# Fetched expert rows turned by column-quarter DMAs and a VectorE transposition, with two smaller edits on TensorE's transposes

## The reference

```python
probs = jax.nn.softmax(x @ router_w, axis=-1)            # 8 experts
gates, idx = jax.lax.top_k(probs, 2)
gates = gates / jnp.sum(gates, axis=-1, keepdims=True)
...
g = jax.nn.silu(x @ w_gate[e]); u = x @ w_up[e]           # for each expert e, 768 x 768
expert_out = (g * u) @ w_down[e]
routed = sum over the two experts of gate * expert_out
shared = jax.nn.silu(x @ ws_gate) * (x @ ws_up) @ ws_down
return alpha * shared + (1.0 - alpha) * routed
```

## Time and profile before

| what | value |
|---|---|
| median of three runs | 1616.88 us |
| time of the profiled execution | 1615.58 us |
| its span | 1613.9 us |
| TensorE busy | 1534.7 us (95%) |
| VectorE busy | 813.6 us (50%) |
| ScalarE busy | 347.2 us (22%) |
| GpSimd busy | 254.3 us (16%) |
| mean granted clock of TensorE | 0.992 of full speed |
| mask blocks | about 477 us to 503 us |
| expert tiles | about 1018 us to 1598 us |

### The profile page before, as it was taken

The page is one execution under the profiler, slowest core; times in us unless marked ns, Lnnn a source line. Parts: engine busy times, 40 slices in busy tenths (PEclk is TensorE's granted clock), DMA queues, the critical chain, the costliest instruction groups (busy, mean ns, idle before and its releaser), DMA issues.

```text
span 1613.9 us, 21893 instructions
## 1 busy us (share of the span) xinstructions
PE 1534.7 (95%) x8432; PEld 1019.5 (63%) x8433; DVE 813.6 (50%) x1534; ACT 347.2 (22%) x525; POOL 254.3 (16%) x236
## 2 busy tenths in 40 slices
PE   5999999999999899999989999899999999999996
PEld 3566676558889899999886555444444444444442
DVE  8655558997677899976897243111111111111111
ACT  3321121112231346550481210110000000001000
POOL 1187820000000000000000047011111111111111
PEclk9999999999999999999999999999999999999998
DMA  9900010000023426213202337924628211613450
GB/s 256 361 2 2 2 62 1 1 1 2 1 60 98 129 76 200 50 25 85 56 23 61 145 88 155 320 92 164 225 79 297 92 49 54 214 40 117 150 204 21
DMA packets 85338, 163.80 MB, mean 101 GB/s; under 512 B 18874, under 2 KB 48816, under 8 KB 85001
## 3 DMA queue, kind: packets, MB, share of 16 engines
q1 hardware_dynamic: 66903, 119.07, 22.9%
q0 software_dynamic: 12096, 23.27, 6.4%
q10 hardware_dynamic: 6258, 20.40, 4.5%
HBM read 127.75 MB, written 37.56 MB: 102 GB/s over the span
## 4 chain that ended last, share of the span: by engine, by line
PE 68%; DVE 11%; POOL 7%; issue 5%; DMA 5%; DVEq 1%; SPq 1%; ACT 1%; POOLq 0%
PE bank L817 30%; PE bank L1641 7%; POOL slot_table L1339 7%; PE bank L1679 6%; PE bank L1600 4%; PE bank L1543 4%; PE bank L727 2%; DVE arena L2412 2%; PE bank L1481 2%; PE bank L737 2%; DVE arena L2381 2%; PE bank L755 2%; PE bank L1727 1%; DMA arena<-in_L_ffn_w_down_dram 1%; DVE arena L2357 1%
## 5 line engine op out<-in xcount | busy, mean ns | idle before, releaser
L817 PE MATMUL bank<-arena 128*64 128x384 f32 x3312 | 539.7, 487 | 3.4 <-DMA arena<-in_L_ffn_w_down_dram 2.8
L817 PEld LDWEIGHTS bank<-arena 128*64 128x64 f32 x3312 | 236.7, 137 | 294.7 <-issue 290.2
L1179 DVE SCALAR_TENSOR_TENSOR arena<-bank,arena 64x384 f32<-64x384 f32 x88 | 50.3, 610 | 356.5 <-DMA arena<-out_dram,arena 216.8
L1679 PE MATMUL bank<-arena 125*125 125x198 f32 (+1 forms) x1200 | 189.2, 318 | 10.6 <-DVE arena L2381 10.5
L1679 PEld LDWEIGHTS bank<-arena 125*125 125x125 f32 x1200 | 182.9, 193 | 14.9 <-DVE arena L2381 14.7
L1641 PE MATMUL bank<-arena 128*125 128x192 f32 x960 | 163.4, 328 | 0.5 <-DVE arena L2334 0.5
L1641 PEld LDWEIGHTS bank<-arena 128*125 128x125 f32 x960 | 157.5, 189 | 0.8 <-DVE arena L2334 0.8
L2221 DVE TENSOR_TENSOR arena<-arena,bank 125x417 f32 x186 | 109.6, 589 | 43.4 <-PE bank L1481 36.2
L1339 POOL DMA_INDIRECT slot_table<-arena x80 | 111.9, 1399 | 93.2 <-issue 93.2
L1543 PE MATMUL bank<-arena 128*125 128x396 f32 x240 | 96.2, 496 | 0.0
L900 ACT ACTIVATE arena<-bank 128x384 f32<-128x384 f32 x46 | 22.6, 492 | 337.0 <-PE bank L817 337.0
(11 more groups left out here) (307 smaller groups left out, 1556.4 us busy)
## 6 DMA issues: line engine op xcount, KB each, us to landing
arena<-in_L_ffn_w_gate_dram SPq DMA_DIRECT2D x9, 2304.0 KB, 8.9
arena<-in_L_ffn_w_up_dram SPq DMA_DIRECT2D x9, 2304.0 KB, 10.8
arena<-in_L_ffn_w_down_dram SPq DMA_DIRECT2D x9, 2304.0 KB, 8.9
arena<-score_rows ACTq DMA_DIRECT2D x18, 585.9 KB
expert_in<-arena SPq DMA_DIRECT2D x23, 384.0 KB, 10.3
arena<-expert_in ACTq DMA_DIRECT2D x23, 384.0 KB, 3.3
arena<-in_L_mix_w_qkv_dram SPq DMA_DIRECT2D x2, 2304.0 KB, 17.7
xn_columns<-arena SPq DMA_DIRECT2D x1, 3750.0 KB, 15.7
```

The costliest lines, as they stand in the source:

```text
L817: ins = tp.matmul(ps[bank][HP * h:HP * h + HP, 0:384], frm[:, b, k, HP * h:HP * h + HP], ew[h][i][:, k, n * 384:(n + 1) * 384], start=(k = ...
L1679: ins = tp.matmul(ps[bank][0:T, c * width:(c + 1) * width], ptile[0:T, j % NPT, dt * T:(dt + 1) * T], values(n - first, st), start=(st == ...
```

## The change

1. **Rows of the experts.** For tiles 1 to 22 the rows are no longer transposed by TensorE. `load_x` issues four DMAs instead of one. DMA number c brings column quarter c (192 columns) of all 128 rows to the 32 partitions 32c to 32c+31; row 32i+r goes to partition 32c+r, place i. One VectorE instruction (`turn_x`) then transposes all 32x32 blocks and writes `xgT` whole. What lands on partition p are then the six features 6p to 6p+5, so the gate and up matrices are laid out in the same way (`"(p k) n -> p k n"`: six consecutive rows of a matrix on a partition, 18 KB in one piece). Down keeps its layout. Tile 0 is still transposed by TensorE, with every sixth column as a piece, and its load is cut in four DMAs by rows. ScalarE's copies of the transposes go.
2. **Transposes of h.** TensorE does those of i=0 inside the second half of the up product (before k=3), and those of i=1 inside the down product (before k=1).
3. **Mask blocks.** ScalarE writes the counts in bf16; TensorE multiplies 125x128 pieces of them with a bf16 identity instead of transposing f32. The three last rows of each result hold other counts and aren't read. VectorE makes the bf16 identity once (one 128x128 copy).

Some semaphores are joined; this moves nothing.

```diff
@@ ffn_sync: the experts' matrices
+        ROWS_OF = ("(p k) n -> p k n", "(p k) n -> p k n", "(k p) n -> p k n")
...
-                sp.dma_start(ew[b][i], w[(NE - 1) * b].rearrange("(k p) n -> p k n", p=P)).then_inc(s_ew[i], 16)
+                sp.dma_start(ew[b][i], w[(NE - 1) * b].rearrange(ROWS_OF[i], p=P)).then_inc(s_ew[i], 16)
...
-                                 w[bass.ds(e, 1)].rearrange("e (k p) n -> p (e k) n", p=P)).then_inc(s_ew[i], 16)
+                                 w[bass.ds(e, 1)].rearrange(("e (p k) n -> p (e k) n", "e (p k) n -> p (e k) n",
+                                                             "e (k p) n -> p (e k) n")[i], p=P)).then_inc(s_ew[i], 16)
@@ ffn_pe: tile
-                pe.wait_ge(s_xTs, 2 * j + 2)
+                if isinstance(j, int) and j == 0:
+                    pe.wait_ge(s_xTs, 2)
+                else:
+                    pe.wait_ge(s_xTd, j)
                 for m in range(2):
                     pe.wait_ge(s_ew[m], loads)
                     for i in range(2):
                         for k in range(KD):
+                            if (m, i, k) == (1, 1, 3):
+                                h_transposes(j, b, 0)
                             ins = product(2 * m + i, xgT, b, k, m, i)
                         ins.then_inc((s_g, s_up)[m], 1)
-                h_transposes(j, b, 0)
-                if not (isinstance(j, int) and j == NTM - 1):
-                    x_transposes(j + 1, 1 - b)
-                else:
+                if isinstance(j, int) and j == NTM - 1:
...
-                h_transposes(j, b, 1)
...
                     if k == 0:
                         pe.wait_ge(s_hTa, j + 1)
+                    if k == 1:
+                        h_transposes(j, b, 1)
@@ ffn_act
             def load_x(j, b):
-                act.dma_start(xgb[:, b], xg_dram[bass.ds(j * P, P)]).then_inc(s_xg[b], 16)
+                rows = xg_dram[bass.ds(j * P, P)].rearrange("(i r) d -> r i d", r=32)
+                for c in range(4):
+                    act.dma_start(xgb[32 * c:32 * c + 32, b].rearrange("p (i d) -> p i d", i=4), rows[:, :, FW * c:FW * c + FW])\
+                        .then_inc(s_xg[b], 16)
...
+                    if not (isinstance(j, int) and j == 0):
+                        act.wait_ge(s_xTd, j)
                     load_x(j + 2, b)
...
-                if not last:
-                    take_x(j + 1, 1 - b)
@@ ffn_dve
+            def turn_x(j):
+                b = j % 2
+                dve.wait_ge(s_xg[b], 64 * (j // 2 + 1))
+                dv.transpose(xgT[:, b].rearrange("p k n -> p (k n)").rearrange("p (k i c) -> p k i c", k=KD, i=4),
+                             xgb[:, b].rearrange("p (i c k) -> p k i c", i=4, k=KD)).then_inc(s_xTd, 1)
+
+            turn_x(1)
             for j in range(NTM - 1):
                 take_h(j)
                 take_hT(j)
+                if j + 2 < NTM:
+                    turn_x(j + 2)
@@ the mask blocks
-                    ins = tp.transpose(ps[(st % 2) * 3 + dt // 4][0:T, (dt % 4) * T:(dt % 4 + 1) * T],
-                                       tbuf[0:T, st % 2, dt * T:(dt + 1) * T], ident[0:T, 0:T])
+                    ins = tp.matmul(ps[(st % 2) * 3 + dt // 4][:, (dt % 4) * T:(dt % 4 + 1) * T],
+                                    countb[0:T, st % 2, dt * T:dt * T + P], ident_b[0:T, 0:T], start=True, stop=True)
...
-                sc.activation(tbuf[0:T, st % 2], counts[0:T, st, 0:N], ACT.Copy).then_inc(s_cf, 1)
+                sc.activation(countb[0:T, st % 2, 0:NW], counts_all[0:T, st * CW:st * CW + NW], ACT.Copy).then_inc(s_cf, 1)
...
+            dv.tensor_copy(ident_b, ident).then_inc(s_kvx, 1)
```

More of the change, by code:

```diff
@@ L143, in gps_layer @@
         token_info = small(4 * NT).rearrange("p (k t c) -> p k t c", k=2, t=NT)
+        ident_b = small(P, BF16)
         u1col = small(NQ)
@@ L271, in gps_layer @@
         tbuf = take(NTB3 * N).rearrange("p (b n) -> p b n", b=NTB3)
+        NW = (NT - 1) * T + P
+        assert (NT - 1) * CW + NW <= 2 * CW16
+        countb = words(SMALL + ZB, NTB3 * N, BF16).rearrange("p (b n) -> p b n", b=NTB3)
         abbuf = take(4 * N).rearrange("p (b s n) -> p b s n", b=2, s=2)
@@ L570, in gps_layer @@
         s_xTs = sem("slot_xT_sb")
+        s_xTd = sem("slot_xT_turned_dve")
         s_h = sem("h_ready")
@@ L795, in ffn_pe, with first_x_transposes @@
             pe.wait_ge(s_sout, 2 * NT)
-            def x_transposes(j, b):
-                wait_use(pe, s_xg[b], j, b, 16)
+            def first_x_transposes():
+                pe.wait_ge(s_xg[0], 64)
                 for i in range(2):
                     for k in range(3):
-                        ins = tp.transpose(ps[6 + i][:, k * P:(k + 1) * P], xgb[:, b, (3 * i + k) * P:(3 * i + k + 1) * P], ident)
-                        if isinstance(j, int) and j == 0 and 3 * i + k < 4 and k < 2 and (i, k) != (1, 1):
+                        ins = tp.transpose(ps[6 + i][:, k * P:(k + 1) * P], xgb[:, 0, 3 * i + k:D:KD], ident)
+                        if 3 * i + k < 4 and k < 2 and (i, k) != (1, 1):
                             ins.then_inc((s_g, s_up, s_y)[2 * i + k], 1)
@@ L883, in ffn_act, with load_first_x, take_first_x @@
                 sc.activation(sg_hT[:, t % 2].rearrange("p k n -> p (k n)"), ps[4 + t % 2][:, 0:KS * T], ACT.Copy).then_inc(s_shTs, 1)
+            def load_first_x():
+                for i in range(4):
+                    act.dma_start(xgb[32 * i:32 * i + 32, 0], xg_dram[32 * i:32 * i + 32]).then_inc(s_xg[0], 16)
             def load_x(j, b):
-                act.dma_start(xgb[:, b], xg_dram[bass.ds(j * P, P)]).then_inc(s_xg[b], 16)
-            def take_x(j, b):
+                rows = xg_dram[bass.ds(j * P, P)].rearrange("(i r) d -> r i d", r=32)
+                for c in range(4):
+                    act.dma_start(xgb[32 * c:32 * c + 32, b].rearrange("p (i d) -> p i d", i=4), rows[:, :, FW * c:FW * c + FW])\
+                        .then_inc(s_xg[b], 16)
+            def take_first_x():
                 for i in range(2):
-                    act.wait_ge(s_slot_xT, 2 * j + 1 + i)
-                    sc.activation(xgT[:, b, 3 * i:3 * i + 3].rearrange("p k n -> p (k n)"), ps[6 + i][:, 0:384],
+                    act.wait_ge(s_slot_xT, 1 + i)
+                    sc.activation(xgT[:, 0, 3 * i:3 * i + 3].rearrange("p k n -> p (k n)"), ps[6 + i][:, 0:384],
                                   ACT.Copy).then_inc(s_xTs, 1)
@@ L902, in tile @@
                 sc.activation(hT[:, b, 0:3].rearrange("p k n -> p (k n)"), ps[0][:, 0:384], ACT.Copy).then_inc(s_hTa, 1)
-                if not last:
-                    take_x(j + 1, 1 - b)
-                else:
+                if last:
                     act.wait_ge(s_h, 2 * j)
@@ L910, in ffn_act @@
             act.wait_ge(s_rows, 16 * 2 * NT)
-            load_x(0, 0)
+            load_first_x()
             load_x(1, 1)
-            take_x(0, 0)
+            take_first_x()
             over_tiles(act, tile)
@@ L1649, in _ @@
             pe.wait_ge(s_mixT, 2 * NT)
+            pe.wait_ge(s_kvx, 2)
             for st in range(NT):
```

31 lines of the change are left out of this document (15 added, 16 removed).

## The result

The changed kernel takes 1629.78 us (median of four runs) where the kernel before, beside it, takes 1616.79: a ratio of 1.0078, 95% interval 1.0059 to 1.0098. It is 13 us slower; the forecast was 4.7 faster. The profiled execution took 1625.59, its span is 1623.9: 10.0 over the span of before.

A forecast was written before the change was run, and what follows sets the result against it. TensorE was taken to bound the kernel. Expert tiles -0.3, mask blocks -4.6 and the bf16 identity +0.2 sum to -4.7, from the median 1616.88 to 1612.2, range 1604 to 1622.

The forecast's parts named there:

- the slower rival: Expert changes: 18 KB weight pieces delay scatter and gather, 2.2 at each of seven changes, 15 in all, 1627; chance 0.20.
- the 5.5: Landing time of GpSimd's two small DMAs beside 30 KB pieces, 2.6 in the quiet; used as evidence against the slower rival.
- More packets for the rows' loads: Expert tiles: the rows' loads send more packets in the same seconds as the gathers, +0.3.
- The +6.1 for stalls: Expert tiles: TensorE waits for h because of late second additions: 2.8 in five tiles, 1.2 behind tile 0, 2.1 in one.
- Tile 0: First expert tile: h transposes inside down are no longer hidden by the 2.79 wait for the down matrix, +0.6.
- The low clock: TensorE's drop to 1.2 GHz behind idle time in the stalled tile: expected the same once more, so no term.
- The last tile: Last expert tile, with one more transpose between up and down: three interruptions for one, +0.3.
- The usual tile: Expert tiles: period of down's starts falls from 24.83 to 24.47, gaining 7.6 over 21 periods.
- the loss of 0.30 for each interruption: Expert tiles: TensorE loses 0.30 where half-width products give way to full-width transposes and come back; two interruptions instead of one.
- switches cost nothing: Rival: transposes' weight loads go ahead of running products, a tile gains 0.94, 1599; free or half free, chance 0.12.
- Mask blocks: Mask stage before the side products: block period falls from 3.04 to 2.53, -4.6 over eight blocks, kept afterwards.
- The earlier deadline of h: Expert tiles: second addition must start within 11.64 of the first, before 13.6; five tiles miss by 0.3 to 0.6.

The follow-up runs named there:

- e3: The changed kernel with each tile's rows fetched by one DMA of 3 KB pieces instead of four, weights still in 18 KB pieces: 1625.25 us, ratio 1.0041.
- e6: The changed kernel with both old DMA forms, 3 KB gate and up pieces and one row transfer: 1614.88 us, ratio 0.9989 to the kernel before.
- e1: The changed kernel with gate and up matrices again in 3 KB pieces, still four row transfers: 1621.27 us, ratio 1.0022 to the kernel before.
- e16: The kernel before with 16-bit mask blocks and h transposes inside the products, x still transposed by TensorE: 1629.61 us, ratio 1.0071.
- e12: The kernel before with gate and up in 18 KB pieces and nothing else changed, transposes reading contiguous columns: 1620.47 us, ratio 1.0008.
- e10: The changed kernel with all old transfers and both groups of h transposes between up and down: 1609.53 us, ratio 0.9953 to the kernel before.
- e5: The kernel before with only the 16-bit mask blocks of the change: 1613.68 us, ratio 0.9979; computes the whole reference.
- e7: The changed kernel, complete, with 3 KB weight pieces, four transfers of 32 partitions per weight matrix, first tile turned on VectorE: 1711.79 us, ratio 1.0579.
- e2: The kernel before with gate and up in 18 KB pieces and TensorE's row transposes reading every sixth column to match: 1624.92 us, ratio 1.0042.
- e9: The kernel before with each tile's rows fetched by four transfers of 768-byte pieces, weights in 3 KB pieces: ratio 1.0028.

## Why the prediction was wrong

**The step that failed** is the dismissal of the slower rival: "the 5.5 does not bear out a cost that grows with the piece". In the sum the 18 KB pieces had no term, and the row transfers only the +0.3 for "More packets for the rows' loads". In the new order the large pieces cost 8.4 to 9 us (e3 against e6, changed against e1), the four row transfers 5.3 to 6 (e1 against e6, changed against e3). The +6.1 for stalls rests on the same step: it takes the first additions as on time and only the second ones as late. The first ones were late by 2.0 to 3.8 at six of seven changes, and the stalls grew by 13.6. Two small DMAs beside 30 KB pieces had stood as evidence for seven chains of scatter and gather.

**The rival's number** was right in part by luck. It named the mechanism, both scatter and gather held up by the pieces, and with 2.2 per change the 1627 is near the measured 1629.78. But its 15 us for the pieces measured 8.4 to 9; it had no row transfers, which gave 5.3 to 6, and it started from 1612.2, where e6, the kernel without either, has 1615.1 by its ratio.

**Tile 0** (+0.6) was mis-sized: its down matrix came only 1.1 earlier though TensorE's first transposes of the stage began 4.6 earlier, so the wait grew to 6.33, and the low clock after it was no term. Part of this belongs to the one execution: the stage's first gate matrix was issued at 999.14 in it, but at 995.84 in e6 and at 996.79 in e1. e6, with all old transfers, still waited 3.27. **The low clock** was "no term" and gave 3.8. **The last tile** (+0.3) has two interruptions more, by the prediction's own 0.30 each 0.6, and grew by 0.9.

**What held.** The usual tile: 24.47 said, 24.48 measured, and the loss of 0.30 for each interruption, shown apart by e16; so the rival "switches cost nothing" is out. Mask blocks: 2.53 and 4.6 said, 2.56 and 4.7 measured in place, 3.4 (interval 1.0 to 5.7) at the end. The transposition was sized 1.1, measured 1.57, and no one waited for it. The earlier deadline of h, with transfers that are not late: stalls of 6.1 more were said; e6, whose transfers are the old ones, has 9.4 for 2.44, 7.0 more, in four places, not seven. With old transfers the whole change gives 0.9989 [0.9972, 1.0007], and the forecast of 0.9971 lies just outside. By e6's profile tile 0 and the low clock are what is left; no run shows it apart.

**The size of the interaction.** Large pieces cost 0.08% in the old order and 0.52% in the new; late h gains twice as much with new transfers as with old, by the medians. The stalls go the same way (7.3 more in e3 than in e6, 4.1 more in e12 than in the kernel before): what had been lateness within the deadline's slack, the time by which h may be late without TensorE standing still, became stalls. So the parts of the change harmed each other. Turning rows on VectorE is worth 0.26%, 4.2 us, where h stays between up and down and transfers are old (e10 against e5). Moving h inside costs 0.36%, 5.8 us (e6 against e10), more than that.

**Open.** Why an 18 KB piece holds up a scatter or a gather more than six pieces of 3 KB do was not measured by itself: e3 and e12 show that it does and by how much, not where a packet waits. Where the four row transfers cost their time isn't shown, nor whether their number, their piece size or their 32 partitions does it. And no kernel here has e10's transfers in a form that computes the reference, so its 1609.5 isn't to be had as it stands.

## What to carry to other kernels

Before a consumer is moved earlier, ask what lateness the old place was hiding, and count the slack of the worst tiles, not of the usual one: here 0.35 us in each of 21 tiles was won, 7.4, and six tiles stalled for 16. Changing a DMA's layout to suit a faster engine changes what every transfer beside it has to wait; price it from a run with the layout alone. Prefer one transfer over all 128 partitions to four over 32: e7 is 5.8% slower by it.

## What the runs showed of the hardware

- With quarters of a weight matrix into 32 partitions in flight the DMA engines moved 214 GB/s, all of them busy (e7); with a whole one into 128 partitions in flight they moved 412 (the kernel before).
- TensorE took 0.81 for six 128x128 transposes whose weights are every sixth f32 (e2), 0.65 for contiguous ones (the kernel before).
- VectorE's transposition of 128x768 f32 in 32x32 blocks took 1.57 reading every sixth number and 0.97 reading runs of 32. The two groups, of the changed kernel and of e7 (count, busy, mean ns, idle before):

```profile
L1215 DVE STREAM_TRANSPOSE arena<-arena 128x768 f32<-128x768 f32 x22 | 34.6, 1572 | 7.3 <-DMA arena<-expert_in 7.3
```
```profile
L1222 DVE STREAM_TRANSPOSE arena<-arena 128x768 f32<-128x768 f32 x23 | 22.3, 969 | 8.8 <-DMA arena<-expert_in 8.8
```

- Behind the waits of 4.84, 5.70 and 6.33 the granted clock fell to 0.50, 1.2 GHz, and behind the 2.44 of before too; behind the five of 1.67 to 2.72 in the changed kernel the next twenty product records kept their 3.45. Behind a wait of 2.29 in e3 three transposes took 0.90, the low clock, and behind the 2.72 in the changed kernel 0.55. So the length of the wait alone doesn't tell it. One such fall cost 2.4 in e9 (144 records in 25.84 for 23.44) and 2.4 in the changed kernel behind the 5.70 (twenty records in 5.53 for 3.45, three transposes in 0.91 for 0.55). It cost about 2.8 behind the 6.33, and 1.4 behind the 2.44 of before.
